# The state-space stage with its carried state on 128 partitions, and a new order of the four engines in a group

## The reference

```python
zxbcdt = u @ W_in.T                       # z 512, x 512, B 64, C 64, dt 4 columns
xBC = silu(causal_conv4(xBC) + b_conv)    # along the tokens
dt = softplus(dt + dt_bias);  A_dt = -exp(A_log) * dt
# per chunk of tokens, head h (4 heads of 128 columns), state of 64 x 128 per head:
Y_diag = (C B^T * Lmat_h) (x_h dt_h)      # inside the chunk
Y_off  = exp(cumsum A_dt) * (C @ state_h) # the readout of the carried state
state_h = exp(sum A_dt) * state_h + (B * decay_h)^T @ (x_h dt_h)   # its update
y = Y + D x;  g = y * silu(z);  out = rmsnorm(g) * norm_w @ W_out.T
```

## Time and profile before

| what | value |
|---|---|
| median of 3 runs | 1299.02 us (1298.74 to 1299.34) |
| profiled execution | 1298.11 us, span of its instructions 1296.2 us |
| mean granted TensorE clock | 0.982 |
| busy, share of the span | PE 95%, DVE 67%, ACT 48%, POOL 34% |
| share of the chain that ended last | PE 86%, DVE 7%, ACT 3%, POOL 2% |

### The profile page before, as it was taken

The page is one execution under the profiler, slowest core; times in us unless marked ns, Lnnn a source line. Parts: engine busy times, 40 slices in busy tenths (PEclk is TensorE's granted clock), DMA queues, the critical chain, the costliest instruction groups (busy, mean ns, idle before and its releaser), DMA issues.

```text
span 1296.2 us, 20859 instructions
## 1 busy us (share of the span) xinstructions
PE 1237.3 (95%) x7112; PEld 1042.1 (80%) x7112; DVE 864.0 (67%) x1654; ACT 618.1 (48%) x1242; POOL 445.8 (34%) x577
## 2 busy tenths in 40 slices
PE   6899999999999999999889999999999899999994
PEld 6777888888888888888757777777777688888884
DVE  4787635454443535344658888889874889999995
ACT  3443323232333323233557878787776544444441
POOL 0345100000000000000157777787775234344443
PEclk8999999999999999999979999999999899999998
DMA  4222101001010101000001001100110101111100
GB/s 179 85 78 86 33 1 33 1 1 33 1 33 1 32 0 49 0 17 1 12 17 37 26 29 38 45 27 25 36 46 17 41 2 33 32 32 32 32 17 33
DMA packets 30393, 41.29 MB, mean 32 GB/s; under 512 B 2432, under 2 KB 22912, under 8 KB 30208
## 3 DMA queue, kind: packets, MB, share of 16 engines
q1 hardware_dynamic: 30336, 40.53, 9.6%
HBM read 27.94 MB, written 12.58 MB: 31 GB/s over the span
## 4 chain that ended last, share of the span: by engine, by line
PE 86%; DVE 7%; ACT 3%; POOL 2%; issue 2%; DMA 0%; POOLq 0%; DVEq 0%; SPq 0%; ACTq 0%; PEldq 0%
PE bank L45 25%; PE bank L47 23%; PE bank L46 23%; PE bank L1825 3%; PE bank L1832 2%; PE bank L1841 2%; PE bank L1773 1%; PE bank L1807 1%; DVE mag L1083 1%; PE bank L1815 1%; PE bank L1748 1%; ACT hh L712 1%; PE bank L1725 1%; PE bank L1726 1%; DVE wf L1091 1%
## 5 line engine op out<-in xcount | busy, mean ns | idle before, releaser
L1159 DVE TENSOR_TENSOR hb<-gl,bank 128x512 f32<-128x512 f32 x128 | 87.8, 686 | 199.2 <-PE bank L47 196.6
L712 ACT ACTIVATE hh<-hb 128x512 fp32r<-128x512 f32 x128 | 80.9, 632 | 182.6 <-DVE hb L1159 182.6
L751 ACT ACTIVATE gl<-bank 128x512 f32<-128x512 f32 x128 | 76.4, 597 | 180.7 <-PE bank L47 180.6
L1122 DVE TENSOR_TENSOR hl<-hb,hh 128x512 fp32r<-128x512 f32 x128 | 95.8, 749 | 84.5 <-ACT hh L712 84.5
L695 POOL TENSOR_TENSOR dhl<-dab,dhh 128x512 fp32r<-128x512 f32 x64 | 96.5, 1529 | 141.4 <-ACT dhh L712 141.4
L540 POOL TENSOR_TENSOR veb<-mvb,eps 128x4 f32<-128x4 f32 x8 | 1.8, 228 | 377.7 <-DVE mvb L1139 377.7
L45 PE MATMUL bank<-xt_l,w_h 128*128 128x512 f32 x256 | 103.9, 406 | 7.2 <-DVE xt_l L1122 4.5
L45 PE MATMUL bank<-at_l,w_hi_a 128*128 128x512 f32 x256 | 102.5, 400 | 0.6 <-PE bank L47 0.3
L47 PE MATMUL bank<-at_h,w_hi_a 128*128 128x512 f32 x256 | 101.9, 398 | 0.0
L47 PE MATMUL bank<-xt_h,w_h 128*128 128x512 f32 x256 | 101.9, 398 | 0.0
L46 PE MATMUL bank<-xt_h,w_l 128*128 128x512 f32 x256 | 101.7, 397 | 0.0
(11 more groups left out here) (233 smaller groups left out, 3655.1 us busy)
## 6 DMA issues: line engine op xcount, KB each, us to landing
xg<-x_scratch SPq DMA_DIRECT2D x16, 512.0 KB, 4.0
xall<-in_x SPq DMA_DIRECT2D x8, 512.0 KB, 6.9
xg<-in_xt SPq DMA_DIRECT2D x8, 512.0 KB, 4.8
x_scratch<-rows_out SPq DMA_DIRECT2D x8, 512.0 KB, 3.1
x_scratch<-rows_out SPq DMA_DIRECT2D x16, 256.0 KB, 2.1
out<-rows_out SPq DMA_DIRECT2D x8, 512.0 KB, 3.2
wq<-in_codes SPq DMA_DIRECT2D x12, 256.0 KB, 2.7
sc<-in_scales SPq DMA_DIRECT2D x12, 256.0 KB, 3.0
```

The lines of the kernel that those rows point to most:

```text
L712: return act.activation(dst, src, ACT.Copy)
L751: act.activation(gl[:, n % 2], ps_gate[n % 2][:], ACT.Gelu_apprx_tanh).then_inc(s_gelu, 1)
L1122: return dve.tensor_tensor(dst, src, hi.bitcast(F32), ALU.subtract)
L1159: dve.tensor_tensor(hb[:, n % 2], gl[:, n % 2], ps_up[n % 2][:], ALU.mult).then_inc(s_h, 1)
```

## The change

The state of a batch lies on 128 partitions: heads 0 and 1 on partitions 0 to 63, heads 2 and 3 on 64 to 127, 2 x 128 columns. The readout becomes two matmuls of 256 columns, one on the upper and one on the lower 64 rows of the array, into two banks (the second half of `ps_ds` is the second); the C rows for the lower one are read where the convolution leaves them. The update becomes four matmuls whose outputs go in turn to partitions 0 to 63 and 64 to 127. VectorE updates the state with two instructions on 128 partitions. The decay sums of the state are computed once for each half. The update waits for the scaled readout of its chunk, since both use `ps_ds`. The calls in `step` stand in another order on TensorE, VectorE, ScalarE and GpSimd, the three shared banks are handed out differently, and the load of the weight piece stands first in SyncE's step. The diff without most of the pure re-ordering on ScalarE, VectorE and GpSimd:

```diff
+        yoff_of = (ps_yoff[:, 0:HALF], ps_ds[:, HALF:2 * HALF])
+        def rows_of(half):
+            return slice(half * D_STATE, (half + 1) * D_STATE)
...
-        T_LANE = (lane_p, lane_r)
+        T_LANE = (lane_q, lane_p)
-        XBC_LANE = (lane_r, lane_p, lane_r, lane_q, lane_r)
+        XBC_LANE = (lane_q, lane_r, lane_q, lane_r, lane_r)
...
-        et = cs("et", [D_STATE, 2, NT, HEADS])
+        et = cs("et", [P, 2, NT, HEADS // 2])
-        state = cs("state", [D_STATE, BATCH, HEADS, HEADDIM])
+        state = cs("state", [P, BATCH, HEADS // 2, HEADDIM])
...
# SyncE, step
+                if more or b == 0:
+                    sp.wait_ge(c_w1l, s + 1)
+                    sp.dma_start(w1_raw[:], w_mlp1[s + 1]).then_inc(c_w1r, 16)
                 if more:
...
-                if more or b == 0:
-                    sp.wait_ge(c_w1l, s + 1)
-                    sp.dma_start(w1_raw[:], w_mlp1[s + 1]).then_inc(c_w1r, 16)
...
# VectorE, new_state
-                for h in range(HEADS):
-                    st = dve.scalar_tensor_tensor(state[:, b, h], state[:, b, h], et[:, b, c, h:h + 1],
-                                                  ps_ds[0:D_STATE, h * HEADDIM:(h + 1) * HEADDIM], ALU.mult, ALU.add)
+                for j in range(HEADS // 2):
+                    st = dve.scalar_tensor_tensor(state[:, b, j], state[:, b, j], et[:, b, c, j:j + 1],
+                                                  ps_ds[:, j * HEADDIM:(j + 1) * HEADDIM], ALU.mult, ALU.add)
...
# VectorE, the new order of step
 cb_mask(k); mixing(k); b_weighted(k); g_lo(k - 1); x2_lo(n, 0), (n, 1); cb_mask(k + 1); add_out(k - 1)
 b_weighted(k + 1); rows_stats(k - 1); mixing(k + 1); y_sum(k); dt_bias_added(n); new_state(k); conv(n, 4)
 dt_one_plus(n); conv(n, 0); b_weighted(k + 2); g_lo(k); cb_mask(k + 2); y_sum(k + 1); new_state(k + 1)
 dt_ratio(n); mixing(k + 2); dt_and_rate(n); add_out(k); conv(n, 1); y_sum(k + 2); new_state(k + 2)
 cb_mask(k + 3); rows_stats(k); mixing(k + 3); g_lo(k + 1); conv(n, 2); y_sum(k + 3); add_out(k + 1)
 b_weighted(k + 3); conv(n, 3); g_lo(k + 2); c_rows(n); rows_stats(k + 1); add_out(k + 2)
 rows_stats(k + 2); new_state(k + 3)
...
# TensorE
+                for half in range(2):
+                    mm = pe.matmul(acs_lane(n)[rows_of(half), 16:24], ones[:], adt[:, :, 2 * half:2 * half + 2], start=True, stop=True)
...
             def in_proj_at(n, j):
                 pe.wait_ge(c_xtl, KT * (n + 1))
-                if j == 0:
-                    pe.wait_ge(c_cv, TAPS * (XB * n + 1))
-                elif j == 1:
-                    pe.wait_ge(c_dtc, DT_STEPS * n + 1)
-                elif j == 2:
-                    pe.wait_ge(c_cv, TAPS * (XB * n + 2))
-                elif j == 3:
-                    pe.wait_ge(c_zs, NT * n + 1)
+                if j == 4:
+                    pe.wait_ge(c_e, NT * n - 1)
+                elif j > 0:
+                    pe.wait_ge(c_cv, TAPS * (XB * n + j))
...
-                pe.matmul(ps_yoff[:], ct[:, b, cols], state[:, b].rearrange("p h d -> p (h d)"),
-                          start=True, stop=True).then_inc(c_yoff, 1)
+                for half, c_rows in ((0, ct[:, b, cols]), (1, bc[rows_of(1), b, cols])):
+                    mm = pe.matmul(yoff_of[half], c_rows, state[rows_of(half), b].rearrange("p h d -> p (h d)"),
+                                   start=True, stop=True)
+                mm.then_inc(c_yoff, 1)
...
             def state_add(k, u):
+                pe.wait_ge(c_yo, k + 1 + 1)
                 pe.wait_ge(c_xsd, k + 1)
                 pe.wait_ge(c_bw, k + 1 + 1)
-                for h in range(HEADS):
-                    mm = pe.matmul(ps_ds[0:D_STATE, h * HEADDIM:(h + 1) * HEADDIM], bw[:, u, h], xsd[:, u, h],
-                                   start=True, stop=True)
+                for j in range(HEADS // 2):
+                    for half in range(2):
+                        mm = pe.matmul(ps_ds[rows_of(half), j * HEADDIM:(j + 1) * HEADDIM], bw[:, u, 2 * half + j],
+                                       xsd[:, u, 2 * half + j], start=True, stop=True)
```

More of the change, by code:

```diff
@@ L929, in step @@
                 x_times_dt(s, b, k + 1, 1, 1)
+                x_token_major(k + 1, 1)
+                if nxt:
+                    xbc_in(n, nb, 4)
+                    dt_exp(n)
+                square(k, 0)
+                if nxt:
+                    xbc_in(n, nb, 0)
+                g_hi(k, 0)
+                y_off(s, b, k + 1, 1, 1)
+                if nxt:
+                    dt_ln(n)
+                segment_exp(s, 3, nxt is not None)
+                if nxt:
+                    conv_silu(n, nb, 4)
+                else:
+                    silu1(0, 0, bank[0], 0)
+                x_times_dt(s, b, k + 2, 2, 0)
+                x_token_major(k + 2, 0)
+                if nxt:
+                    xbc_in(n, nb, 1)
+                    conv_silu(n, nb, 0)
+                else:
+                    silu1(0, 1, bank[0], 1)
+                square(k + 1, 1)
+                y_off(s, b, k + 2, 2, 0)
+                if nxt:
+                    z_silu(n, 0)
+                    xbc_in(n, nb, 2)
+                x_token_major(k + 3, 1)
+                x_times_dt(s, b, k + 3, 3, 1)
+                if nxt:
+                    conv_silu(n, nb, 1)
+                g_hi(k + 1, 1)
+                if nxt:
+                    xbc_in(n, nb, 3)
+                else:
+                    silu1(0, 2, bank[0], 0)
+                y_off(s, b, k + 3, 3, 1)
                 if before:
@@ L1394, in step @@
                     gated1(0, 0, 0, bank[1])
+                b_weighted(k + 2, 2, 0)
+                g_lo(k, 0)
+                cb_mask(k + 2)
+                y_sum(k + 1, 1)
+                new_state(s, b, k + 1, 1)
+                if nxt:
+                    dt_ratio(n)
+                mixing(k + 2, 2, 0)
+                if nxt:
+                    dt_and_rate(n, nb)
                 add_out(s, b, k, 0, 0)
@@ L1705, in decay_sums @@
             def decay_sums(n):
-                pe.wait_ge(c_cv, TAPS * XB * (n + 1))
+                if isinstance(n, int) and n == 0:
+                    pe.wait_ge(c_cv, TAPS * XB)
+                else:
+                    pe.wait_ge(c_zs, NT * n + 3)
                 pe.wait_ge(c_dtc, DT_STEPS * (n + 1))
                 flat = adt[:].rearrange("p t h -> p (t h)")
-                pe.matmul(ACS_LANE[:, 0:16], upto[:], flat, start=True, stop=True)
-                pe.matmul(ACS_LANE[0:D_STATE, 16:32], ones[:], flat, start=True, stop=True).then_inc(c_acs, 1)
+                pe.matmul(acs_lane(n)[:, 0:16], upto[:], flat, start=True, stop=True)
+                for half in range(2):
+                    mm = pe.matmul(acs_lane(n)[rows_of(half), 16:24], ones[:], adt[:, :, 2 * half:2 * half + 2], start=True, stop=True)
+                mm.then_inc(c_acs, 1)
             def segment_sums(n, t, more=True):
@@ L1720, in segment_sums @@
                 elif t == 2 and more:
[L1721 removed]
+                    pe.wait_ge(c_e, NT * n + 1)
+                elif t == 2:
+                    pe.wait_ge(c_zs, NT * (n + 1))
+                elif more:
+                    pe.wait_ge(c_dtc, DT_STEPS * (n + 1) + 1)
                 else:
[L1723 removed]
+                    pe.wait_ge(c_e, NT * n + 3)
                 pe.wait_ge(c_au, 2 * (NT * n + t + 1))
@@ L1853, in step @@
                 n, nb, ni = nxt if nxt else (None, None, None)
+                segment_sums(s, 1)
                 pe.wait_ge(c_silu, XB * s + turn(s, HEADS) + 1)
                 pe.wait_ge(c_ct, s + 1)
-                y_off(k, b, 0)
+                scores_cb(k, b, 0)
                 if nxt:
                     x2_turn(n, nb, ni, 0)
-                scores_cb(k, b, 0)
+                segment_sums(s, 2, nxt is not None)
+                if before:
+                    g_transpose(k - 1, 1)
+                y_off(k, b, 0)
+                scores_cb(k + 1, b, 1)
                 if nxt:
```

243 lines of the change are left out of this document (95 added, 148 removed).

## The result

The changed kernel takes 1286.95 us (median of 4 runs, 1285.0 to 1287.65) beside 1299.18 of the kernel before (4 runs in the same session): a ratio of 0.9904, 95% interval 0.9889 to 0.992, or 12.2 us less. The forecast was 25.7 us less. The profiled execution took 1287.44 us, with a span of 1285.2.

A forecast was written before the change was run, and what follows sets the result against it. TensorE's own work was taken to bound each 42.8 us step. Shape changes and tiles, 2.8 us a step (22.7 over 8 steps), plus 3 at the entry gave 25.7 us off 1299.0: 1273 us, range 1262 to 1292.

The forecast's parts named there:

- The changes of shape: TensorE, steady step: 21 instead of 26 changes of the stationary operand's shape, taken as 0.7 us a step.
- half the time for the state update: VectorE: two instructions on 128 partitions replace four on 64, saving 2 us a step, leaving about 35 us.
- ScalarE's copies unchanged: ScalarE: the four scaled copies of the readout keep their size, 0.372 us each, only reading two banks.
- The entry: Start of the stage: segment sums, scores and transposes fill TensorE's 4.83 us standstill; 3 us gained, between 2 and 5.5.
- a change of tile: Rival, 5%: in readout and update it costs as much as a change of shape, 20 us over 32 chunks; 1310 us.
- a slip: Rival, 6%: the convolution before input projection 3 comes late as VectorE meets GpSimd more often; 1306 us at 2 us a step.
- Passes in this trace always start in program order: TensorE's tiles: partial overlap, readout three lengths (gain 0.21 us), update five (gain 0.32), for each chunk.
- the upper bound of the sum: TensorE's gain with both tile halves fully side by side: 0.7 + 4 x 0.86 = 4.1 us a step, 33 us in all.
- the 15% rival: Full overlap of the tiles on TensorE: 4.1 us a step, less some 0.5 of waits for VectorE; 1267 us; 15%.
- zero net: Steady step: a loss at VectorE's meeting is set against the old 0.2 us wait for the gated rows' low part.
- the tightest meeting: Input projection 3, needing the convolution of piece 1: TensorE 15.4 us, VectorE 15.0 starting 0.2 later, so 0.2 us early.
- the rival without overlap: Tiles on TensorE don't overlap; only shape changes and the entry remain, 5.6 + 3 = 8.6 us; 1290 us; 18%.

The follow-up runs named there:

- e1: The changed kernel with state, readout, update and decay sums as before the change, so the new order alone: 1298.64 us, ratio 1.0006.
- e3: The changed kernel with VectorE's dt ratio and rate steps moved behind the output sum of chunk 0 and convolution 1: 1281.22 us, ratio 0.9871.
- e10: The changed kernel with one long tap instruction of every convolution piece cut to 4 columns, leaving a tap out of the result: 1276.47 us.
- e8: The kernel before with the tiles in its old order, and ScalarE's scaled readout of chunk 0 first in its step: 1284.7 us, ratio 0.9896.
- e6: The changed kernel with ScalarE's first silu of the last MLP put ahead of the square of chunk 0 in the last step: 1282.21 us.
- e2: The kernel before with the tiles alone, in the old order, and the update's wait for the scaled readout: 1309.24 us, ratio 1.0093.
- e5: The changed kernel with VectorE's dt steps behind the state update of chunk 2, and GpSimd's gating of chunk 2 before the rates split: 1287.04 us.
- e7: The changed kernel with GpSimd's low part of the weight piece moved from behind the gating of chunk 0 to behind chunk 2's: 1289.06 us.
- e11: e9 with ScalarE's copy of the gated rows of chunk 2 put ahead of four other calls: 1280.37 us, ratio 0.9861.
- e13: e9 with ScalarE's copy of the gated rows of chunk 2 and silu of z 2 ahead of the residual copy and a norm: 1279.69 us.
- e9: The changed kernel with the moves of e3 and e6 together: 1277.78 us, ratio 0.9847.
- e4: The changed kernel with the four matmuls of an update in the order upper, upper, lower, lower half: 1286.64 us (one run).

## Why the prediction was right in direction and twice too large

**Right.** The changes of shape: 0.7 us forecast, 0.67 measured (e1). VectorE: half the time for the state update, and 35.7 us a step for a forecast 35. ScalarE's copies unchanged. The entry: segment sum at 650.79, readout at 655.15, clearing 0.52 instead of 0.94 us, and a first interval 5.3 us shorter for a forecast 5.8 (3 and one step), within its spread. No price on a change of tile: the two of a pair start 7 ns apart and the pairs 0.11 us, so that rival is out. The mechanism named for a slip, meetings of VectorE with GpSimd in front of input projection 3, came, for the smaller of the two waits.

**Wrong, the tiles.** The step "Passes in this trace always start in program order" priced a readout at three lengths and an update at five, 0.53 us a chunk together. Both overlap fully, 0.86 a chunk. TensorE's need fell by 4.2 us a step (42.8 to the estimated 38.6), not by 2.8; the upper bound of the sum was 4.1. This alone would have made the time shorter than forecast; the 15% rival had the right mechanism.

**Wrong, the waits: "zero net" (with full overlap some 0.5 a step).** They are 1.76 us of idle time, 2.2 in slots. Two errors made them. VectorE's stretch was put at 15.0 us and took 17.0: the first convolution instruction takes 1.22 us instead of 0.16, a later dt step (L1287) 0.92 instead of 0.17, the rest are short gaps between dependent instructions. And the prediction took input projection 3 for the tightest meeting and has no sum for the one just ahead of it in the queue, the transposes of chunk 1 waiting for the output sum of chunk 0: the larger wait, 1.12 us. e3 takes the ratio steps off both meetings and gains 5.7 us; e10 gives VectorE 0.7 us a convolution piece and gains 10.5. So steady steps gave 2.02 us each and not 2.84: 4.9 us of the missing 14.6 (25.7 - 11.1).

**Wrong, the exit: not costed at all.** The prediction multiplied the step's gain by 8 steps, and the last of them isn't like the others, since work of the last MLP stands where the next group's stood. There the tail grew by 6.4 us where the sum had it fall by 2.8: 9.2 us, the larger part of the error. e1 and e8 show that this is the order's doing: the tail is 8.6 us longer with the new order alone, and 2.4 shorter with the tiles in nearly the old one. What it is made of is 5.7 us more of idle time and two more stretches at the lower clock. e6, one call moved on ScalarE, gives 3.8 us of it back, mostly as clock. The other waits of the last step weren't tried one by one, and their causes stay open.

So in all: order, -4.0 in six steps, -4.1 at the front, +8.6 at the exit, which is nothing; and the tiles, which make the whole difference: of their 27 us (8 x 3.4) less than half arrived.

That the time still lies in the stated range (1262 to 1292) is luck: tiles worth more than the sum had and waits that it lacked came together, and 1287 us lies nearer to the rival without overlap (1290), whose mechanism is wrong, than to the forecast.

## What to carry to other kernels

When an engine without slack becomes faster, sum the whole queue of the next engine up to each meeting, not only to the one that looks tightest, and count the collisions; the first and the last step of a pipeline get sums of their own. Two parts of a change should be priced as if each were alone: here one call moved in ScalarE's queue (24.5 us between e2 and e8) did as much for the tiles as the new order of four engines. And look for the wait that a fix uncovers before making it: of five moves in the steady step (e3, e5 and e7 on the changed kernel, e11 and e13 on e9) one gained, and the others turned a wait into one at another place.

## What the runs showed of the hardware

- Float32 matmuls on different tiles of one shape ran side by side pass by pass, their starts 7 ns apart on row tiles and on column tiles, and also where two matmuls of the same tile are neighbours in the program (e4: 13 ns, four lengths for eight passes).
- VectorE instructions on 3 or 16 columns with their inputs in SBUF, 0.15 to 0.17 us alone, lasted 0.42 to 1.22 us where they began during a GpSimd instruction on 512 or 768 columns, and ended 0.02 to 0.04 us after it. The state update, with one input in PSUM, kept its length in the same place.
- Idle times of 1.55 to 2.2 us of TensorE in an otherwise busy stretch were followed by 3.4 us at the lower granted clock, but not each time: in e2 in four of the six steady steps with the same 2.2 us wait; in the changed kernel's last step behind 2.12, 1.55 and 1.83 us and not behind 1.33 and 0.67; and in e9's behind none, with 1.55 and 1.83 us in it. So their length alone doesn't decide it.
